# Softmax attention on one Trainium2 core: two score tiles in neighbouring PSUM banks, one VectorE instruction for both row maxima

## What is computed

```python
qkv = (x @ w_qkv).reshape(b, n, 3, H, DK)          # H = 16 heads of DK = 8
q, k, v = ...                                        # b, h, n, d
attn = jnp.einsum('bhnd,bhmd->bhnm', q, k) * (1.0 / np.sqrt(DK))
attn = jax.nn.softmax(attn, axis=-1)
y = jnp.einsum('bhnm,bhmd->bhnd', attn, v)
x = x + y.transpose(0, 2, 1, 3).reshape(b, n, d) @ w_proj
```

## Time and profile before

| | us |
|---|---|
| median of 3 runs | 712.17 (711.34 to 712.18) |
| the profiled execution, its own time | 712.04 |
| its span (first to last instruction) | 709.9 |

### The profile page before, as it was taken

One profiled execution on the slowest core, in us unless ns is written; L12 is line 12 of the kernel. 1 busy time (PEld: TensorE's weight loads), 2 busy tenths in 40 slices (PEclk: granted clock), 3 DMA queues, 4 the chain that ended last, 5 costly groups with the idle time before them and its releaser, 6 DMA issues.

```text
span 709.9 us, 16403 instructions
## 1 busy us (share of the span) xinstructions
PE 632.1 (89%) x5448; PEld 330.1 (46%) x5448; DVE 586.2 (83%) x1296; ACT 493.9 (70%) x1007; POOL 424.1 (60%) x965
## 2 busy tenths in 40 slices
PE   4599789989977898999999999999999998977994
PEld 2367556666655222223333333322323323877994
DVE  5877998998867988899999999999999964645552
ACT  3634666676554378888889888888888888524662
POOL 6212657667555754346676777878878736543553
PEclk9899999999999689999999999999999999978998
DMA  6564134235253221146200303012030003615500
GB/s 181 178 211 127 60 91 141 102 117 179 90 181 112 68 90 46 45 124 206 68 24 12 102 24 112 13 46 85 19 113 13 24 35 95 188 69 154 146 31 12
DMA packets 42898, 66.25 MB, mean 93 GB/s; under 512 B 7948, under 2 KB 36335, under 8 KB 39808
## 3 DMA queue, kind: packets, MB, share of 16 engines
q1 hardware_dynamic: 39232, 56.73, 26.3%
q0 software_dynamic: 3296, 8.41, 3.3%
q10 hardware_dynamic: 288, 0.07, 0.0%
HBM read 41.64 MB, written 22.26 MB: 90 GB/s over the span
## 4 chain that ended last, share of the span: by engine, by line
PE 62%; ACT 16%; DVE 10%; issue 6%; POOL 3%; SPq 1%; another core or an unknown queue 1%; DMA 1%; POOLq 0%; DVEq 0%; ACTq 0%
PE bank L1087 14%; PE pair L1076 9%; ACT arena L1999 8%; PE bank L1048 7%; PE pair L1337 5%; PE bank L1098 3%; DVE arena L1572 3%; PE pair L1346 2%; PE bank L1346 2%; PE bank L942 2%; ACT arena L1968 2%; DVE arena L1408 2%; PE bank L931 2%; POOL arena L654 2%; PE pair L1128 2%
## 5 line engine op out<-in xcount | busy, mean ns | idle before, releaser
L1999 ACT ACTIVATE arena<-pair 128x512 f32<-128x512 f32 x506 | 277.9, 602 | 49.1 <-PE pair L1076 46.3
L1572 DVE TENSOR_REDUCE arena<-bank 128x1 f32<-128x512 f32 x388 | 251.8, 684 | 7.8 <-PE bank L1048 6.4
L1076 PE MATMUL pair<-q_stack,k_stack 64*128 64x512 bf16 x506 | 158.2, 386 | 6.4 <-ACT arena L1999 5.1
L1048 PE MATMUL bank<-k_stack,q_stack 63*128 63x512 bf16 x388 | 136.8, 395 | 7.0 <-DVE arena L1572 4.1
L1087 PE MATMUL bank<-arena,values 128*9 128x512 f32 x1024 | 133.9, 595 | 1.6 <-ACT arena L1999 1.5
L1408 DVE TENSOR_TENSOR arena<-bank,cst 128x512 f32<-128x512 f32 x128 | 82.0, 682 | 24.6 <-PE bank L916 24.1
L1572 DVE TENSOR_REDUCE arena<-pair 128x1 f32<-128x512 f32 x124 | 84.5, 682 | 1.8 <-PE pair L1048 1.4
L719 POOL TENSOR_TENSOR arena<-arena 128x32 f32<-128x32 f32 (+6 forms) x312 | 68.8, 220 | 24.4
L1048 PEld LDWEIGHTS bank<-k_stack,q_stack 63*128 63x128 bf16 x388 | 33.1, 93 | 106.6 <-ACT arena L2004 25.8
L1076 PEld LDWEIGHTS pair<-q_stack,k_stack 64*128 64x128 bf16 x506 | 40.6, 93 | 49.2 <-ACT arena L1999 24.3
L2135 ACT ACTIVATE fq_all<-pair 128x512 f32<-128x512 f32 x39 | 23.3, 596 | 40.9 <-PE pair L1337 27.7
(11 more groups left out here) (298 smaller groups left out, 1249.1 us busy)
## 6 DMA issues: line engine op xcount, KB each, us to landing
softmax_parts<-arena SPq DMA_DIRECT2D x8, 768.0 KB, 4.1
q_stack<-softmax_parts SPq DMA_DIRECT2D x48, 128.0 KB
k_stack<-softmax_parts SPq DMA_DIRECT2D x48, 128.0 KB
linear_parts<-arena SPq DMA_DIRECT2D x7, 768.0 KB, 3.7
q_stack<-linear_parts SPq DMA_DIRECT2D x42, 128.0 KB
k_stack<-linear_parts SPq DMA_DIRECT2D x42, 128.0 KB
arena<-in_L_ffn_w_dram SPq DMA_DIRECT2D x16, 256.0 KB, 4.5
v_all<-token_rows SPq DMA_DIRECT2D x20, 192.5 KB, 2.5
```

What stands on the lines that cost most here:

```text
L1048: pe.matmul(bank[:], qs[b % 2][rows, slot, qt * P:(qt + 1) * P], ks[b % 2][rows, slot, :], start=True, stop=True).then_inc(d_s_m, 1)
L1076: pe.matmul(score_bank(s)[:], ks[u][rows, 2 * g + x, kt * P:(kt + 1) * P], qs[u][rows, 2 * g + x, :], start=True, stop=True).then_inc(d_s_ ...
L1572: dve.reduce_max(mx[:, m % 2, col:col + 1], bank[:], AX).then_inc(d_s_mr, 1)
L1999: act.activation(pt[:, kt % 2, x, half, :], score_bank(s)[:], ACT.Exp, scale=SCALE).then_inc(d_s_e, 1)
```

## The change

All eight banks become one PSUM tensor `psum` of 128 x 8 x 512, so that neighbouring banks can be addressed by one instruction. `k.bank` is numbered anew: the ring is physical banks 0 to 3 in a row (before: bank0, bank1, bank3 and the first half of pair0), and `b_num` moves to bank 4.

In step `kt`, max0 and max1 stand in ring places `kt` and `kt + 1`. For `kt` = 0, 1 and 2 these are neighbours, and one TENSOR_REDUCE over 128 x 2 x 512 takes both maxima. It waits for max1 (`x + 2`), and counts `d_s_mr` up by two when it ends. For `kt` = 3 the places are 3 and 0, and two single reductions stay. PE's and ACT's instructions and waits stay as they were.

```diff
-        k.bank = [top.enter_context(nc.psum_tensor(f"bank{i}", [P, 4 * P], F32)) for i in range(4)]
-        k.pair = [top.enter_context(nc.psum_tensor(f"pair{i}", [P, 8 * P], F32)) for i in range(2)]
-        k.bank += [k.pair[0][:, 0:512], k.pair[0][:, 512:1024], k.pair[1][:, 0:512], k.pair[1][:, 512:1024]]
+        k.psum = top.enter_context(nc.psum_tensor("psum", [P, 8, 4 * P], F32))
+        k.bank = [k.psum[:, i, :] for i in (0, 1, 4, 2, 3, 5, 6, 7)]
...
+        def ring_pair(n, kt):
+
+            i = (n * C + kt) * USES % len(ring)
+            if i == len(ring) - 1:
+                return None
+            return k.psum[:, i:i + 2, :]
...
+                def two_maxima(m, x, banks):
+                    col = x // 4
+                    dve.wait_ge(d_s_m, m * 16 + x + 2)
+                    dve.reduce_max(mx[:, m % 2].rearrange("p (h c) -> p h c", h=2)[:, :, col], banks, AX).then_inc(d_s_mr, 2)
+
...
                 for n in range(NB):
                     for kt in range(C):
                         if n + 2 < NB:
+                            banks = ring_pair(n, kt)
                             for j in range(4):
-                                maximum(n + 2, 4 * kt + j, ring_bank(n, kt, j))
+                                if banks is None or j > 1:
+                                    maximum(n + 2, 4 * kt + j, ring_bank(n, kt, j))
+                                elif j == 0:
+                                    two_maxima(n + 2, 4 * kt, banks)
                                 if j == 1:
                                     late_piece(n, kt)
                                 if n >= 10 and n % C == 2 and 4 * kt + j < 7:
```

## The result

The changed kernel takes 718.84 us in the median of 5 runs (716.35 to 720.0), against 712.17 (711.34 to 712.76) before: 1.0096 times as long, with a 95% interval of 1.0081 to 1.0110. It is slower, as forecast, but by 6.7 us instead of 2.8, which is outside the range of 711.3 to 718.5. Its profiled execution has a span of 716.7 us against 709.9. Four of its five executions had a mean granted clock of 0.961, and the fastest, 716.35 us, had 0.967.

The account below looks back on a forecast made before the run. The prediction took a loop of PE, ACT and DVE waiting on each other as the bound, not DVE's total work. Terms 1.33 + 0.08 + 1.35 = 2.76 us took the median of 712.17 to 714.9 us, range 711.3 to 718.5.

Parts of the forecast that it names:

- the loop: Ordinary head group: PE, ACT and DVE waiting on each other set 10.55 us; DVE in it only from 475.72 to 479.29.
- DVE's busy share of 19.89 in 20 us: Softmax stage: a rival took DVE's work as setting the pace, 5.4 us gained, 706.8 us; chance 0.10.
- slack of 0.04 ahead of max2 of step 1: Ordinary group: max2 waited for ACT, its own release ready at about 473.96, so 0.04 of step 0's delay is absorbed.
- step 1: Ordinary group: the pair does not wait, and its gain of 0.06 ends in idle time before the reduction at 475.72.
- the price of a pair: Merged reduction on DVE: 1.14 us to the next start, length near 1.22, saving 0.06 a pair.
- third rival: Merged pairs: the second bank costs an instruction's worth, 1.20 a pair, nothing saved, 6.2 us slower, 718.4 us; chance 0.13.
- figure of 125 ns an instruction: DVE on PSUM: by the skill's cost a pair would take some 1.08, and the estimate would be near 711 us.
- the release, 0.04 us behind max1: Step 0, ordinary group: the pair starts 0.04 behind max1's end, at 471.61, 0.19 later than before.
- the forecast's -0.02: Step 2, ordinary group: arriving 0.09 late, the pair takes 1.15 instead of 1.20; the fourth reduction is 0.07 late.
- the sum had 1.4: Ordinary groups: 19 at 0.07 us longer each, plus groups 4 and 5 at 0.04 each, 1.33 + 0.08.
- groups 4 and 5: Groups with a narrower addition and a shorter wait for max0: put at half, 0.04 us longer each.
- groups with small instructions: The five groups with `choose`: 0.27 us longer each, 11.35 to 11.62, two exposed results adding 0.12 and 0.14; 1.35 in all.

Follow-up runs that it names:

- e3: Changed kernel with merged pairs in step 0 alone, against the kernel before the change: 719.33 us, ratio 1.0099.
- e5: Changed kernel with merged pairs in step 2 alone, against the kernel before the change: 713.86 us, ratio 1.0009.
- e4: Changed kernel with merged pairs in step 1 alone, against the kernel before the change: 712.94 us, one run.
- e13: Changed kernel with each merged reduction counting d_s_mr up by one and PE's waits renumbered: 716.58 us, ratio 1.0046 to the kernel before.
- e15: Changed kernel counting by one, with merged pairs only from group 1 on: 716.03 us, ratio 1.0053 to the kernel before.
- e11: Changed kernel with the merged reduction reading only the first 256 columns of each of its two banks: 707.04 us, one run.
- e7: Merging in step 2 alone, of max1 and max2, banks renumbered, PE's order as in the kernel before: 711.54 us, ratio 1.0002 to that kernel.
- e12: Changed kernel with the merged reduction reading its first bank twice, 1024 columns from one bank: 718.87 us, one run.
- e8: Changed kernel with merged pairs only from group 1 on: 718.65 us, ratio 1.0075 to the kernel before.

## Why the prediction was right and wrong

**Right: the direction, and the loop.** DVE's busy share of 19.89 in 20 us did not count. The loop through step 0, ACT, step 1, the normalisation and step 2 did, with its slack of 0.04 ahead of max2 of step 1. e3 gave 0.15 in step 0, which is 0.25 - 0.06 - 0.04; e5 gave 0.04 in step 2, and e4 none in step 1. The forecast had step 1 right in its sum, though with the real lag the pair there is held up a little by its release.

**Right: the price of a pair.** Spacing 1.14 and length 1.22, from the slope of two reductions. The third rival gave 718.4, close to the result, but its mechanism is refuted: the second bank costs nothing beyond its columns. An estimate from the figure of 125 ns an instruction in the Trainium skill (Perfetto Trace Analysis, "Optimizing Scalar/DVE Operations") made the pair 1.08; the trace shows 1.14.

**Wrong: the release, 0.04 us behind max1.** This is the step "so the pair starts at 471.61, 0.19 behind the 471.42 of before". The lag was read from a single reduction and carried over to an instruction that differs in one thing I had not priced, its count of two. It was 0.105. In an ordinary group this term stands twice: the pair of step 0 came 0.25 late instead of 0.19, which made 0.15 instead of 0.09, and that of step 2 0.10 behind DVE's readiness instead of 0.03, which made 0.04 instead of the forecast's -0.02. Together 0.19 instead of 0.07, times 21: 4.0 us, where the sum had 1.4. e13, which has the forecast's lag, gives 10.60 where 10.62 was forecast. Its time is 3.3 us over the kernel before, where 2.8 was forecast, but that near agreement is partly luck: in its profile the ordinary groups cost 1.2 us (1.4 forecast) and those with small instructions 2.2 (1.35 forecast).

Of the 2.6 us between 4.0 and 1.4 the lag accounts for some 2.4, and the rest is groups 4 and 5, which I had put at half and which lost the full 0.19. In the groups with small instructions the lag of step 0 adds 0.3. With the lag alone put right the forecast would have been some 717.6, inside its range. What lifted the measurement out of it is the 1.6 of group 0 and the rest of what the groups with small instructions cost, against -0.9 elsewhere.

**Nearly right: groups with small instructions.** The second small one stood 0.21 behind the first, as worked out (group 22, changed kernel; the sixth stands 0.24 behind the fifth, not 0.39, since the fifth took 0.35 in group 10 and 0.21 here):

```profile
500.10 0.17 DVE L1613 TENSOR_REDUCE d_top<-h_all 128x4 f32<-128x32 f32 x1
500.31 0.19 DVE L1615 TENSOR_TENSOR d_equal<-h_all,d_top 128x32 f32<-128x32 f32 x1
...
502.94 0.21 DVE L1622 TENSOR_TENSOR d_onehot<-d_equal,d_top 128x32 f32<-128x32 f32 x1
503.18 0.24 DVE L1625 TENSOR_TENSOR_SCAN d_counts<-d_carry,d_onehot 128x40 f32<-128x40 f32 x1
```

Four of the groups lost 0.28 to 0.38 where 0.27 was forecast. They took 11.58 to 11.64, near the 11.62 forecast; the groups before, of which I had read one, took 11.20 to 11.36. Group 14 lost 0.76, with DVE idle for 0.61 before its pair:

```profile
411.32 1.23 DVE L1583 TENSOR_REDUCE arena<-psum 128x2 f32<-128x1024 f32 x1 [0.61 <-PE psum L1054]
```

That is 0.35 more than the release explains. The longer spacing recurs at this group in the versions that merge in step 0 with the count of two, and not in those that count by one; its cause is open.

The versions that count by one took longer in other groups. e13's five took 11.55, 11.51, 11.82, 11.81 and 11.81. In the last three the second small instruction took twice its time (groups 10 and 22):

```profile
368.14 0.19 DVE L1629 TENSOR_TENSOR d_equal<-h_all,d_top 128x32 f32<-128x32 f32 x1
...
498.42 0.39 DVE L1629 TENSOR_TENSOR d_equal<-h_all,d_top 128x32 f32<-128x32 f32 x1
```

It is the same in e15. So these groups cost about as much without the late release as with it, and the price of a small instruction that was laid bare is not as steady as the forecast took it to be. Why it takes longer there is not shown.

**Not in the sum: group 0.** I counted 0 for groups 0 to 3, from DVE's idle time in 280 to 300 us, which lies in groups 2 and 3. It held for 1 to 3. In group 0 the profile shows 1.6, with the clock, as above. The clock was no term of the sum at all. e11 and e13 say that the wait itself costs next to nothing there; whether the change had a part in the longer stretch of low clock stays open.

## What to carry to other kernels

Before merging two instructions, ask when the merged one can start: it waits for the later of its inputs, and where the engine was already waiting for the first, the delay is paid in full while the saving is only the fixed part, here 0.06 us against 0.19. Merge where the engine has a queue: the same instruction placed behind a busy stretch saved its 0.06 in every ordinary group, though no gain in the kernel's time could be shown. And when an edit removes n instructions but the total in the page's head does not fall, look for what came in: a wait that stood inside an instruction may have become one of its own.

## What the runs showed of the hardware that I had not expected

- A reduction of DVE that waits and counts its semaphore by two has its wait as a separate instruction of 21 ns on the queue, and where it has to wait it starts 0.105 us behind the matmul that releases it; counting by one (e13), the wait is inside, and it starts 0.04 behind. The two came and went together, so how much of the 0.07 is the separate instruction itself is not shown. Where DVE was busy at the release, the separate wait cost nothing: e7 has 30 of them, and its pairs start with no gap. Whether the chip or the making of the program demands the separate wait, the runs do not tell.
- In these versions a reduction's time went by its columns, not by its banks or outputs: 1.14 us to the next for 1024, over two banks or twice over one (e12), 0.61 for 512, over one bank or two (e11), each behind a wait.
- The stretch of low granted clock near 237 us varies in length between executions whose instructions there are the same (0.66 in e15 and 0.59 in e8 over 25 us), and with it group 0 by 1.0 us: as much as some of the edits studied.
